# A two-layer graph network in 40,000 hand-ordered instructions: own step lists for the first and the last rounds, and a fifth staging buffer for the weights

## The reference

```python
h = jnp.maximum(_layernorm(x), 0.0)
x = x + _L0_gnn_ref(h, adj, adj, Wq, Wk, Wv, bv, Wo, bo)   # 12-head attention, bias 2*adj
h = jnp.maximum(_layernorm(x), 0.0)
x = x + _L1_gnn_ref(h, adj, W_left, W_right, W_lin, b_lin, ln_a, ln_b)
```

## Time and profile before

| | us |
|---|---|
| median of 3 runs (lowest, highest) | 1509.23 (1505.95, 1509.36) |
| profiled execution | 1507.34 |
| its span, first to last instruction | 1505.4 |
| PE busy, share | 1432.3, 95% |
| PE's weight loads | 1396.4, 93% |
| DVE | 1243.8, 83% |
| ACT | 903.5, 60% |
| POOL | 508.9, 34% |

### The profile page before, as it was taken

The page is one execution under the profiler, slowest core; times in us unless marked ns, Lnnn a source line. Parts: engine busy times, 40 slices in busy tenths (PEclk is TensorE's granted clock), DMA queues, the critical chain, the costliest instruction groups (busy, mean ns, idle before and its releaser), DMA issues.

```text
span 1505.4 us, 40241 instructions
## 1 busy us (share of the span) xinstructions
PE 1432.3 (95%) x14464; PEld 1396.4 (93%) x14464; DVE 1243.8 (83%) x4619; ACT 903.5 (60%) x2027; POOL 508.9 (34%) x921
## 2 busy tenths in 40 slices
PE   3699999999999999999999999999999999999874
PEld 3599999999999999999999999999999999999874
DVE  5578988888888888888888888888888888888853
ACT  4566665656666556666565666656666665566531
POOL 4113333233334233343323333333333342333321
PEclk8799999999999999999999999999999999999996
DMA  6232322223221223232222333222223222232200
GB/s 216 54 57 58 68 42 62 48 64 68 57 62 43 55 60 64 58 67 50 55 50 61 68 57 68 41 57 53 64 68 57 56 49 57 58 64 57 54 12 11
DMA packets 235683, 89.39 MB, mean 59 GB/s; under 512 B 206784, under 2 KB 235200, under 8 KB 235488
## 3 DMA queue, kind: packets, MB, share of 16 engines
q1 hardware_dynamic: 234912, 85.63, 26.9%
q0 software_dynamic: 576, 1.18, 0.3%
HBM read 23.86 MB, written 12.58 MB: 24 GB/s over the span
## 4 chain that ended last, share of the span: by engine, by line
PE 92%; DVE 2%; DMA 2%; ACT 1%; issue 1%; POOL 1%; SPq 0%; DVEq 0%; POOLq 0%; ACTq 0%
PE bank L342 79%; PE bank L348 4%; PE bank L415 4%; PE bank L403 3%; PE bank L422 1%; DMA x_sb<-x 1%; DMA pT<-prob_parts 1%; PE bank L434 0%; ACT prob L507 0%; SPq L323 0%; DVE weights L570 0%; ACT xn L490 0%; DVE stats_ln L598 0%; ACT prob_parts L515 0%; ACT work L556 0%
## 5 line engine op out<-in xcount | busy, mean ns | idle before, releaser
L342 PE MATMUL bank<-h,weights 128*128 128x256 f32 x3456 | 425.1, 280 | 3.0 <-DVE h L750 3.0
L342 PEld LDWEIGHTS bank<-h,weights 128*128 128x128 f32 x3456 | 411.9, 190 | 3.8 <-issue 3.7
L507 ACT ACTIVATE prob<-prob,rmin 128x128 f32<-128x128 f32 x768 | 244.2, 393 | 3.4 <-DVE rmin L665 3.4
L342 PE MATMUL bank<-weights,h 128*128 128x384 f32 x1152 | 227.5, 342 | 0.0
L342 PE MATMUL bank<-hA,weights 128*128 128x256 f32 x1728 | 219.2, 283 | 1.4 <-DVE hA L585 1.4
L342 PEld LDWEIGHTS bank<-hA,weights 128*128 128x128 f32 x1728 | 212.1, 190 | 1.7 <-DVE hA L585 1.7
L342 PEld LDWEIGHTS bank<-weights,h 128*128 128x128 f32 x1152 | 194.3, 188 | 6.3
L483 ACT ACTIVATE n<-bank 128x512 fp32r<-128x512 f32 x192 | 113.7, 592 | 141.7 <-PE bank L342 141.0
L800 POOL TENSOR_SCALAR less_mean_gnn<-mv_gnn 128x2 f32<-128x2 f32 x64 | 32.9, 513 | 429.9 <-DVE mv_gnn L590 429.9
L665 DVE CUSTOM_DVE_ANT_0 prob<-bank,adj_sb 128x128 f32<-128x128 f32 x768 | 171.0, 286 | 0.2 <-issue 0.2
L585 DVE TENSOR_TENSOR n<-bank,n 128x512 fp32r<-128x512 f32 x192 | 128.9, 684 | 33.8 <-ACT n L483 28.9
(11 more groups left out here) (101 smaller groups left out, 2453.8 us busy)
## 6 DMA issues: line engine op xcount, KB each, us to landing
x_sb<-x SPq DMA_DIRECT2D x32, 384.0 KB, 3.2
out<-x SPq DMA_DIRECT2D x32, 384.0 KB, 2.7
adj_sb<-adj SPq DMA_DIRECT2D x32, 128.0 KB, 2.1
pT<-prob_parts SPq DMA_TRANSPOSE x256, 2.8
x<-w SPq DMA_DIRECT2D x3, 576.0 KB, 4.8
pT<-w SPq DMA_DIRECT2D x3, 576.0 KB, 6.6
prob<-w SPq DMA_DIRECT2D x2, 576.0 KB, 7.3
prob_parts<-w SPq DMA_DIRECT2D x2, 576.0 KB, 6.0
```

The costliest lines, as they stand in the source:

```text
L342: mm = pe.matmul(out, lhsT, rhs, start=(n == 0), stop=(n == len(pairs) - 1))
L507: e = act.activation(prob[:, a * C + h // HC, :], prob[:, a * C + h // HC, :], ACT.Exp, bias=rmin[:, j, h:h + 1], scale=-1.0)
```

## The change: own lists for the first and last rounds

`program(engine)` becomes `HEAD` (a list of (step, group) for what the rounds -2 to 1 held), 27 rounds of the unchanged `ORDER` (first = 2 to 28), and `TAIL` (a list of (step, group - NG) for what the rounds 29 to 32 held). `BANK` and `ORDER` are as before. The setup's work becomes steps of the lists: `w0` to `w9` on SP (load), ACT (HI) and DVE (LO), `const` on DVE, `setup`, `loadv` and `loads` on POOL. The beginnings and ends of the lists (the full ones have some 100 steps for PE):

```diff
+HEAD = {
+    "SP": [
+        ("ld_x", 0), ("w0", 0), ("ld_x", 1), ("w1", 0), ("w2", 0), ("w3", 0), ("ld_adj", 0), ("ld_adj", 1), ("w4", 0),
+        ("w5", 0), ("w6", 0), ("w7", 0), ("w8", 0), ("pth01", 0), ("ptl01", 0), ("pth00", 0), ("ptl00", 0), ("w9", 0),
+        ("pth11", 0), ("ptl11", 0), ("pth10", 0), ("ptl10", 0), ("ld_adj", 2), ("ld_x", 2), ("ptl01", 1), ("pth00", 1),
...
+    "PE": [
+        ("S01", 0), ("T1a", 0), ("T1b", 0), ("S02", 0), ("QK1", 0), ("QK0", 0), ("QK2", 0), ("V0", 0), ("S00", 0), ("S03", 0),
+        ("V1", 0), ("S11", 0), ("T1b", 1), ("S12", 0), ("S10", 0), ("S13", 0), ("T1a", 1), ("AT", 0), ("QK0", 1), ("PV0", 0),
+        ("QK1", 1), ("QK2", 1), ("V0", 1), ("OT0", 0), ("PV1", 0), ("WO0", 0), ("OT1", 0), ("V1", 1), ("WO1", 0), ("S02", 1),
+        ("S00", 1), ("S01", 1), ("S03", 1), ("T2b", 0), ("T2a", 0), ("N02", 0), ("N01", 0), ("N00", 0), ("S12", 1), ("S10", 1),
...
+    "ACT": [
+        ("w0", 0), ("xn1_1", 0), ("xn1_0", 0), ("w1", 0), ("T1a", 0), ("w2", 0), ("T1b", 0), ("w3", 0), ("w4", 0), ("w5", 0),
+        ("QK1", 0), ("QK0", 0), ("w6", 0), ("QK2", 0), ("xn1_0", 1), ("xn1_1", 1), ("w7", 0), ("x03", 0), ("x02", 0),
+        ("ph01", 0), ("x01", 0), ("x00", 0), ("T1b", 1), ("ph00", 0), ("T1a", 1), ("V0", 0), ("V1", 0), ("w8", 0), ("x13", 0),
+        ("x12", 0), ("ph11", 0), ("x10", 0), ("x11", 0), ("ph10", 0), ("w9", 0), ("AT", 0), ("QK1", 1), ("QK2", 1), ("QK0", 1),
+        ("OT0", 0), ("V0", 1), ("OT1", 0), ("V1", 1), ("x02", 1), ("xn2_0", 0), ("xn2_1", 0), ("x03", 1), ("T2b", 0),
...
+    "DVE": [
+        ("ln1_st", 0), ("ln1_ag", 0), ("ln1_st", 1), ("ln1_ag", 1), ("w0", 0), ("w1", 0), ("T1a", 0), ("T1b", 0), ("w2", 0),
+        ("w3", 0), ("w4", 0), ("w5", 0), ("QK1", 0), ("QK0", 0), ("QK2", 0), ("w6", 0), ("va0", 0), ("S03", 0), ("S02", 0),
+        ("S01", 0), ("w7", 0), ("S00", 0), ("pl01", 0), ("va1", 0), ("S13", 0), ("T1b", 1), ("pl00", 0), ("T1a", 1), ("S10", 0),
+        ("S12", 0), ("S11", 0), ("V0", 0), ("V1", 0), ("r00", 0), ("pl11", 0), ("PV0.r", 0), ("PV0.n", 0), ("PV0.o", 0),
+        ("const", 0), ("pl10", 0), ("w8", 0), ("w9", 0), ("r01", 0), ("va0", 1), ("QK0", 1), ("OT0", 0), ("PV1.r", 0),
+        ("PV1.n", 0), ("PV1.o", 0), ("WO0", 0), ("V0", 1), ("OT1", 0), ("QK2", 1), ("QK1", 1), ("va1", 1), ("WO1", 0),
+        ("ln2_st", 0), ("ln2_ag", 0), ("S02", 1), ("S01", 1), ("S03", 1), ("ln1_st", 2), ("S00", 1), ("r00", 1), ("T2b", 0),
...
+    "POOL": [
+        ("ln1", 0), ("ln1", 1), ("ml", 0), ("setup", 0), ("loadv", 0), ("loads", 0), ("xbo0", 0), ("xbo0", 1), ("xbo1", 0),
...
+TAIL = {
...
+        ("HL11", -3), ("AT", -2), ("N01", -2), ("C11", -3), ("C10", -3), ("N02", -2), ("S11", -1), ("S10", -1), ("N00", -2),
+        ("S12", -1), ("S13", -1), ("HL00", -2), ("U0", -2), ("HL01", -2), ("PV0", -1), ("C01", -2), ("C00", -2), ("OT0", -1),
+        ("PV1", -1), ("WO0", -1), ("OT1", -1), ("HTb", -2), ("HTa", -2), ("WO1", -1), ("N10", -2), ("N11", -2), ("N12", -2),
+        ("HL10", -2), ("T2a", -1), ("U1", -2), ("T2b", -1), ("HL11", -2), ("AT", -1), ("N01", -1), ("C10", -2), ("C11", -2),
+        ("N02", -1), ("N00", -1), ("HL00", -1), ("U0", -1), ("HL01", -1), ("C00", -1), ("C01", -1), ("HTb", -1), ("HTa", -1),
+        ("N10", -1), ("N11", -1), ("N12", -1), ("HL10", -1), ("U1", -1), ("HL11", -1), ("C10", -1), ("C11", -1)],
...
+        ("HL00", -1), ("U0.m", -1), ("U0.w", -1), ("U0.d", -1), ("U0.dh", -1), ("U0.dl", -1), ("HL01", -1), ("y0", -2),
+        ("y1", -2), ("C00", -1), ("C01", -1), ("gst00", -1), ("gst01", -1), ("gag0", -1), ("HTb.h", -1), ("HTb.l", -1),
+        ("HTa.h", -1), ("HTa.l", -1), ("N10", -1), ("N11", -1), ("N12", -1), ("U1.m", -1), ("U1.w", -1), ("HL10", -1),
+        ("U1.d", -1), ("U1.dh", -1), ("U1.dl", -1), ("HL11", -1), ("C10", -1), ("C11", -1), ("gst10", -1), ("gst11", -1),
...
+FIRST, LAST = 2, 3
...
-        return [(step, first + ahead) for first in range(-AHEAD, NG + BEHIND) for step, ahead in ORDER[engine] if 0 <= first + ahead < NG]
+        rounds = [(step, first + ahead) for first in range(FIRST, NG - LAST) for step, ahead in ORDER[engine]]
+        return HEAD[engine] + rounds + [(step, NG + back) for step, back in TAIL[engine]]
```

The staging tiles are five: the second half of `qk` joins them, and the weights are spread anew. A weight's load waits for the split of the one that had its tile before. The waits of group 0 that guarded the staging tiles are set one by one:

```diff
-        LOADS = ((0, 0), (1, 1), (2, 2), (3, 3), (4, 0), (5, 1), (6, 2), (7, 3), (8, 0), (9, 1))
+        LOADS = ((0, 2), (1, 3), (2, 1), (3, 0), (4, 2), (5, 3), (6, 1), (7, 0), (8, 4), (9, 0))
...
-                    pp[:, :, :, :].rearrange("p s h q -> p (s h q)").bitcast(F32)[:, 0:C * H])[STAGE_OF[m]]
+                    pp[:, :, :, :].rearrange("p s h q -> p (s h q)").bitcast(F32)[:, 0:C * H],
+                    qk[:, 1, :, :, :].rearrange("p s c t -> p (s c t)").bitcast(F32)[:, 0:C * H])[STAGE_OF[m]]
...
                     if g == 0:
-                        sp.wait_ge(s_wlo, NW)
+                        sp.wait_ge(s_wlo, 7)
...
                 elif step[:2] == "QK":
                     k = int(step[2])
+                    if g == 1:
+                        act.wait_ge(s_wlo, 9)
...
                     ge(act, s_turned[HI][b], 16 * (G * g + j))
+                    if g == 0:
+                        act.wait_ge(s_wlo, 6)
...
                     dve.wait_ge(s_xin[p], 16 * (n + 1))
+                    ge(dve, s_aggr["ln1"], g)
...
                     if g == 0:
-                        dve.wait_ge(s_cload, 16 * CONST_LOADS)
+                        dve.wait_ge(s_bvload, 16)
...
                     if g == 0:
-                        dve.wait_ge(s_wlo, 8)
+                        dve.wait_ge(s_wlo, 5)
...
+                    if g == 0:
+                        dve.wait_ge(s_wlo, 6)
                     dve.wait_ge(s_part[HI][b], G * g + j + 1)
...
                     ge(dve, s_out[p], 16 * n)
+                    if g == 0:
+                        dve.wait_ge(s_wlo, NW)
```

More of the change, by code:

```diff
@@ L112 @@
 }
+HEAD = {
[18 rows of a table added]
+        ("HTb", 1), ("HTa", 1), ("V1", 3)],
+    "ACT": [
[13 rows of a table added]
+        ("OT1", 2), ("HTb", 1), ("HTa", 1)],
+    "DVE": [
[20 rows of a table added]
+    "POOL": [
[3 rows of a table added]
+}
+TAIL = {
[17 rows of a table added]
+    "ACT": [
[14 rows of a table added]
+    "DVE": [
[26 rows of a table added]
+    "POOL": [
[4 rows of a table added]
+}
+FIRST, LAST = 2, 3
 SPLIT_JOBS = (["T1a", "T1b", "QK0", "QK1", "QK2",
@@ L117 @@
               [f"HL{l}{j}" for l in range(L) for j in range(G)])
-CONST_LOADS = 6 + 2 * C
-AHEAD = max(ahead for steps in ORDER.values() for _, ahead in steps)
-BEHIND = -min(ahead for steps in ORDER.values() for _, ahead in steps)
+CONST_LOADS = 5 + 2 * C
 def build(nc, x_d, adj_d, w_d, bias_d, bo_d, lna_d, lnb_d, out_d):
@@ L240, in build @@
         ones_zeros = work[:, 3 * P:3 * P + 4 * G].rearrange("p (s g k) -> p s g k", s=2, g=G)
-        LOADS = ((0, 0), (1, 1), (2, 2), (3, 3), (4, 0), (5, 1), (6, 2), (7, 3), (8, 0), (9, 1))
+        LOADS = ((0, 2), (1, 3), (2, 1), (3, 0), (4, 2), (5, 3), (6, 1), (7, 0), (8, 4), (9, 0))
         STAGE_OF = dict(LOADS)
-        SPLIT_AFTER = {
-            "ACT": {"": (0,), "xn1_1": (1,), "T1b": (2, 3), "QK1": (4, 5), "QK0": (6,), "QK2": (7,), "V0": (8,), "V1": (9,)},
-            "DVE": {"ln1_ag": (0,), "T1b": (1, 2), "QK1": (3, 4), "QK0": (5,), "QK2": (6, 7), "V0": (8,), "V1": (9,)}}
         def staged(m):
@@ L292, in _ @@
         def _(sp):
-            def load_weights(ms):
-                for m in ms:
-                    if m >= 4:
-                        sp.wait_ge(s_wlo, m - 3)
-                    sp.dma_start(staged(m), w_d[m].rearrange("(c p) o -> p c o", p=P)).then_inc(s_wload[STAGE_OF[m]], 16)
             def run(step, g):
                 p, n = g % 2, g // 2
-                if step == "ld_x":
+                if step[0] == "w":
+                    m = int(step[1])
+                    before = [k for k in range(m) if STAGE_OF[k] == STAGE_OF[m]]
+                    if before:
+                        sp.wait_ge(s_wlo, before[-1] + 1)
+                    sp.dma_start(staged(m), w_d[m].rearrange("(c p) o -> p c o", p=P)).then_inc(s_wload[STAGE_OF[m]], 16)
+                elif step == "ld_x":
                     for j in range(G):
@@ L330, in _ @@
                 run(step, g)
-                if g == 0 and step == "ld_x":
-                    load_weights(range(4))
-                if g == 0 and step == "ld_adj":
-                    load_weights(range(4, NW))
             for p in range(2):
@@ L486, in run @@
                 p = g % 2
-                if step[:4] == "xn1_":
+                if step[0] == "w":
+                    m = int(step[1])
+                    wait_load(act, m)
+                    act.activation(W[:, m, HI, :, :], staged(m), ACT.Copy, scale={WQ: Q_SCALE, WK: K_SCALE}.get(m, 1.0)).then_inc(s_whi, 1)
+                elif step[:4] == "xn1_":
                     j = int(step[4])
@@ L753, in _ @@
                 run(step, g)
-                if g == 0:
-                    split_weights(SPLIT_AFTER["DVE"].get(step, ()))
```

(14 more changed lines are left out.)

33 lines of the change are left out of this document (15 added, 18 removed), and 83 rows, old and new, of tables (HEAD, TAIL).

## The result

The changed kernel takes 1494.5 us in the median of 4 runs (1493.6 to 1495.5), the kernel before 1507.6 in 4 runs: ratio 0.9909, 95% interval 0.9896 to 0.9921. It is faster by 13.1 us. I had said 1490, which is 17.6 us less than that median; 1482 to 1499 was the range. The profiled execution took 1495.5, its span 1493.4.

What follows compares the result with a forecast made beforehand. PE was taken to bound the middle, with waiting at both ends: 1507.3 less 16.0 (head) less 2.5 (tail) is 1488.8, and half of the profiled execution's 1.9 us offset puts the median at 1490; range 1482 to 1499.

Steps and rivals of the forecast that it cites:

- forecast A: Main forecast: group 0's second-norm transpose (T2) between 52 and 61 us, total time 1483 to 1496; chance 0.72.
- What bounds: PE bounds the middle at 44.22 us a round; 90 us of the span, mostly at both ends, aren't its work.
- First S: Head: group 0's first score step at 23.5 us, 13.6 us earlier, as fewer splits stand ahead and x loads early.
- From S to T2: Head, first score step to group 0's second-norm transpose: PV1 at 43.5, then 12 us, T2 at 55.5, gain 16.0.
- My sign of being wrong: Head: the forecast would be wrong if the second graph's score steps came over 9 us after the first's.
- Behind T2: From group 0's second-norm transpose to group 1's second-layer projections: same work, 2.7 us slow clock kept, no change.
- The tail: Last rounds: earlier U0 and moved y steps bring C00's eviction about 1.8 us forward; 2.5 together, bounds 0 and 4.
- The fifth tile: Head staging tile: ACT's group 1 QK steps wait for nine splits; 2 to 3 us late, hidden before PV1.
- B: Rival, head: DVE nearly without idle, gain 20 to 24 us, time 1480 to 1485; chance 0.09.
- C: Rival, head: constants issued late on POOL delay WO1's eviction; gain 8 us less, time 1498; chance 0.10.
- D: Rival, head: QK and V stay at 1.2 GHz, 16 to 20 us on the path; 1505 to 1509; chance 0.05.
- E: Rival, loop: PE waits once each round, slower; 1521 at 1.2 us a round; chance 0.04.

Runs made afterwards that it cites:

- r3: Kernel before with one load moved: x of group 1 goes out behind the first weight; ratio 0.9979 to the kernel before, 3.2 us faster.
- r8: Changed kernel with own tiles for the transposed probabilities of group 0's second graph; ratio 0.9908 to the kernel before.
- r10: Changed kernel with own tiles for group 0's second-graph transposed probabilities plus extra PE matmuls in head and tail; ratio 0.9874 to the kernel before, median 1489.1 us.
- r9: Changed kernel itself, timed again; ratio 0.9914 to the kernel before; its profile is the second profile.
- r2: Changed kernel with the last four rounds taken from the old list (new head alone); ratio 0.9935 to the kernel before, 9.8 us faster.
- r5: Changed kernel without the fifth staging tile, tenth weight loaded later; ratio 0.9938 to the kernel before.
- r6: Changed kernel with 24 extra PE matmuls ahead of T2 and 7 ahead of N02 of group 0; ratio 0.9907 to the kernel before, median 1494.0 us.
- r12: r5 (no fifth staging tile) run again beside the changed kernel; ratio 0.9917 to the kernel before, the changed kernel beside it 0.9914.
- r4: Changed kernel with the constants' DMAs issued right behind group 0's norm, in place of behind the weights; ratio 0.9933 to the kernel before.
- r7: r6 (changed kernel, extra matmuls in the head) with extra matmuls also in three PE idle stretches of group 31; ratio 0.9887 to the kernel before.
- r11: r10 with 14 extra matmuls ahead of T1a and 12 ahead of QK0 of group 1; ratio 0.9853 to the kernel before, median 1485.9 us.
- r1: Kernel before with the new lists for the last four rounds only; ratio 0.9986 to the kernel before, 2.1 us faster.

## Why the prediction was right, and where it was short

The time lies inside the range and T2 inside forecast A, and the mechanism was the one described. The sizes were less good than the total: I had said 16.0 us for the head, nothing behind T2 and in the loop, and 2.5 for the tail, and the spans say 11.8, a loss of 2.15 and one of 1.3, and 3.6. The tail's 1.1 us too much, which made up for part of the head's shortfall, was luck: the last N1 at a better clock alone gave 1.0.

**What bounds.** Right. All gain is ahead of T2 of group 0 and behind N1 of group 29; the loop's rounds stayed at 44.22 us, with a longer one now and then in both kernels. One sum in this part was wrong: the pieces of work ahead of 150.19 add up to 102.4 us and not 103.5, so that 47.8 and not 46.7 would be waiting. The forecast doesn't use it.

**First S** was forecast for 23.5 and came at 23.8 (24.7 in the second profile). The parts held too: x of group 1 in at 7.2, the first split at 8.39 (8.8), PE's first QK at 12.32 (12.9), the eighth weight's wait of 1.67 us inside the bound of 1 to 2. But my reading of the kernel before named only one of its two long waits. Ahead of the first score step DVE was busy for 21.1 of 37.1 us before and for 15.1 of 23.8 after. So 6.0 of the 13.3 us are work, nearly all of it steps that no longer stand ahead (three splits, one value add and two value steps), and 7.3 are idle time. The wait for x, 3.49 us, is less than half of that; r3 takes it away and gains 3.2. A larger one I didn't mention, though my sum filled it: DVE waited 4.52 us for the first QK eviction.

```profile
18.64 0.69 DVE L585 TENSOR_TENSOR qk<-bank,qk 128x512 f16<-128x512 f32 x1 [4.52 <-ACT qk L483]
```

In the new lists the fifth and sixth split stand there, and DVE idles 0.58 and 0.60 us ahead of them. That these splits gave the rest of the gain is read from the trace; no run has them alone.

**From S to T2** was forecast as 32 us and took 35.9 and 33.5 in the two profiles. The step that failed is PV1 at 43.5, which came at 46.7 and 46.5. Two terms of it were too small. First, I counted one transpose's issue and landing behind the last split. But all four of the second graph wait until PV0 has read pT, and are then issued one behind another. PE was done with its own work at 44.8 and waited 1.86 us for the last one; in r8 and r10, with tiles of their own, that wait is 0. Second, PV0 came late. I had QK0 start 9.0 us behind the first S and take 2.6 us (54 matmuls in 7.88). It started 10.2 us behind it and took 3.7 in the first profile, and 8.9 and 4.2 in the second. The late start goes with the probability split that took 1.79 us beside POOL: I had priced POOL beside DVE at 0.8 us on a weight split, and it came on this step, which is in the chain. My sign of being wrong, S of the second graph more than 9 us after the first, was met in part: its first step came 5.7 us behind, the other three 9.5 (5.3 and 8.1 in the second profile).

WO0 at the low clock was another 1.3 us of the first profile: it took 3.12 us there at a granted clock of 0.53, behind 1.86 us of idle ahead of PV1, and 1.84 in r9 at 1.00, behind 1.53. r2, r5, r6 and r12 are like the first (2.45 to 3.23 us behind 1.68 to 2.02), r4 and r7 like the second (1.83 and 1.84 behind 1.15 and 1.10).

T2 comes at 55.95 in r11, beside the 55.5 of my sum, but with extra matmuls that the forecast didn't have.

**Behind T2** I had taken no change. It was 2.15 us, in the second profile 1.8. I had moved 2.7 us of slow clock along unchanged. But the scores of group 1, which stood between T2 and N0 and kept PE busy there, now stand ahead of the idle. So PE had 38 matmuls less to do in this stretch and yet was busy as long as before (78.73 and 78.70 us), N0 taking 8.84 us at a granted clock of 0.72, and it idled 2.1 us more, 1.46 of it right ahead of N0. r6, r7, r10 and r11 fill the idle, and N0 takes 6.40: this step is shown. The bound of some 5 us that I had set for the clock in the head was the right term; I had left it out of the sum itself. N1 of group 1, forecast at 134, came at 140.5 and 138.7.

**The tail** was forecast at 2.5; the spans say 3.6 and 3.8, r1 alone 2.1 by its times. U0 came 1.6 us earlier against N1 of group 30, as worked out (1.5). The moved y steps gave nothing: the sum of the two masked scores now fell beside a POOL operation and took 1.20 us in place of 0.42. N1 of group 30 to that of 31 gained 1.5 us, and this stands in every profile with the new tail (1.1 to 2.4 where no matmuls were added). Group 29 to 30, forecast at 0, gave 0.9, but over the profiles it is 42.5 to 44.0 us with the new tail and 43.4 to 44.0 with the old one, so this isn't steady. The last stretch gave 1.2, of which 1.0 is N1 by its clock (9.21 to 8.23); r2 and r3 have it with the old tail, so it isn't the change's.

**The fifth tile** and the constants were forecast as no part of the gain. For the tile the times agree (r12, 0.9917 beside 0.9914), though the profiles without it are some 1 us longer up to T2. The constants' place moved the first scores by 1.8 to 2.7 us (r4); what it does to T2 and to the whole stays open.

**The rivals.** B and C did not come: the issues of the constants on POOL took 0.54 us each beside the splits, that of the value bias 0.77. D, the clock, was a matter of degree: the head's mean clock was 0.90 and 0.92, and it took an estimated 4 to 5 of the 18.5 us (2.4 in N0, 1.1 to 1.6 in QK0 against 2.6, 1.3 in WO0 where it fell there). E did not come.

**Open.** The stretch from group 1 to group 29 took 1239.8 to 1241.6 us in the eleven profiles with the new head, and 1239.1 to 1239.7 in the three with the old one. The extra is spread over some rounds of 44.3 to 45.4 us, not the same ones in each profile, and I haven't found its cause.

## What to carry to other kernels

When the bound engine is full in the middle, sum the two ends against the middle's pace and look for the first event behind which it never idles again: what brings it forward brings the rest forward, less what is taken back behind it (here 2.15 of 11.8 us, by idle time and a lower clock). Work ahead of that event is in pieces, so count its matmuls at the clock that the profile shows for such pieces, and for a group of transfers that wait for the same buffer count every issue, not the last one. A few matmuls without use in PE's idle stretches were worth some 4 us here (r7), while taking away the remaining buffer wait alone gave nothing that the times can show (r8). And the same program moved by 2 to 3 us between executions up to one event, so look at several profiles before a difference of that size is put down to a change.
